# Six row buffers, earlier token numbers and four zero products in the capacity MoE of a four-layer block

## What is computed

```python
logits = x @ gate_weight.T                        # 128 experts
logits = where(old_to_new == -1, -inf, logits)    # 48 are kept
top_v, top_i = top_k(softmax(logits), 8)
top_v = top_v / sum(top_v)
pos = (running count of the tokens of the same expert) - 1
valid = pos < 96                                  # CAP slots for each expert
xb[e, pos] = x[token]                             # gather
h = silu(xb @ Wg[e]) * (xb @ Wu[e])               # 96 inner columns
out = h @ Wd[e]
final[token] += out[e, pos] * weight * valid      # combine
```

## Time and profile before

| what | value |
| --- | --- |
| median of 3 runs | 1504.42 us |
| the profiled execution's own time | 1502.56 us |
| its span, first to last instruction | 1500.7 us |
| PE busy | 1265.7 us (84%) |
| DVE busy | 1178.3 us (79%) |
| ACT busy | 758.1 us (51%) |
| POOL busy | 762.9 us (51%) |
| mean granted TensorE clock | 0.789 |
| layer 3's quads, first to last silu (ACT L1573) | 727.37 to 854.78 us of the span |

### The profile page before, as it was taken

One profiled execution on the slowest core, in us unless ns is written; L12 is line 12 of the kernel. 1 busy time (PEld: TensorE's weight loads), 2 busy tenths in 40 slices (PEclk: granted clock), 3 DMA queues, 4 the chain that ended last, 5 costly groups with the idle time before them and its releaser, 6 DMA issues.

```text
span 1500.7 us, 30682 instructions
## 1 busy us (share of the span) xinstructions
PE 1265.7 (84%) x11448; PEld 778.8 (52%) x11448; DVE 1178.3 (79%) x2410; ACT 758.1 (51%) x1457; POOL 762.9 (51%) x727
## 2 busy tenths in 40 slices
PE   6878999999996999974798873888888889993798
PEld 3544555555553333233687761555555655562455
DVE  7858777777769999977787569888888767659784
ACT  4442222222236988863343334988999943331432
POOL 5444767676611005000332246988988947773262
PEclk9999999999997555557799995555555589996899
DMA  6120111111013999981556524998999921110010
GB/s 215 43 78 32 43 52 42 52 42 52 21 36 65 173 180 174 176 168 41 142 173 173 162 50 84 143 152 145 149 151 150 141 71 40 46 54 31 12 33 28
DMA packets 350670, 143.14 MB, mean 95 GB/s; under 512 B 328912, under 2 KB 331472, under 8 KB 349776
## 3 DMA queue, kind: packets, MB, share of 16 engines
q1 hardware_dynamic: 347232, 132.88, 42.7%
q0 software_dynamic: 1728, 4.72, 1.1%
q10 hardware_dynamic: 1584, 3.86, 0.8%
HBM read 59.09 MB, written 2.10 MB: 41 GB/s over the span
## 4 chain that ended last, share of the span: by engine, by line
PE 50%; DVE 27%; POOL 6%; ACT 5%; issue 5%; DMA 5%; SPq 1%; ACTq 0%; POOLq 0%; DVEq 0%
PE s_all L863 32%; DVE small L2250 7%; PE bank L863 6%; PE s_all L1072 2%; PE bank L1072 2%; POOL c_hi L772 2%; PE s_all L1254 2%; DVE stats L1791 1%; DVE small L2253 1%; POOL c_hi L770 1%; POOL c_lo L772 1%; PE s_all L977 1%; DVE ffbuf L2092 1%; PE bank L1389 1%; DVE xt_lo L1812 1%
## 5 line engine op out<-in xcount | busy, mean ns | idle before, releaser
L619 POOL TENSOR_TENSOR w_hi<-w_in,ws_col 128x768 f16<-128x768 f32 (+1 forms) x76 | 109.6, 1442 | 268.4 <-PE bank L863 259.5
L863 PE MATMUL s_all<-xt_hi,w_hi 128*128 128x512 f16 x576 | 172.5, 381 | 17.2 <-DVE ffbuf L2061 7.1
L2063 DVE TENSOR_TENSOR hid_lo<-ffbuf,hid_hi 128x512 f16<-128x512 f32 x80 | 142.2, 1778 | 56.4 <-ACT hid_hi L1501 56.4
L620 POOL TENSOR_SCALAR w_in<-w_in 128x768 f32<-128x768 f32 (+1 forms) x76 | 182.8, 2405 | 0.0
L1501 ACT ACTIVATE hid_hi<-ffbuf 128x512 f16<-128x512 f32 x80 | 50.4, 630 | 247.8 <-DVE ffbuf L2061 247.8
L863 PE MATMUL s_all<-xt_lo,w_hi 128*128 128x512 f16 x576 | 172.8, 382 | 0.0
L863 PE MATMUL s_all<-xt_hi,w_lo 128*128 128x512 f16 x576 | 172.4, 381 | 0.0
L1639 ACT ACTIVATE ag<-s_all,small 128x1024 int16<-128x1024 f32 x128 | 154.0, 1203 | 23.8 <-DVE small L2253 13.5
L2250 DVE TENSOR_REDUCE small<-s_all 128x1 f32<-128x1024 f32 x128 | 155.5, 1215 | 7.3 <-PE s_all L1254 7.2
L665 POOL DMA_INDIRECT sel<-rows,slot_misc x36 | 43.4, 1204 | 204.9 <-DVE slot_misc L1949 130.6
L1254 PE MATMUL s_all<-ag 32*128 32x512 f16 x256 | 131.5, 616 | 12.2 <-ACT ag L1639 7.4
(11 more groups left out here) (387 smaller groups left out, 3210.9 us busy)
## 6 DMA issues: line engine op xcount, KB each, us to landing
w_in<-in_w_blocks SPq DMA_DIRECT2D x76, 384.0 KB, 3.0
w_in<-in_w_experts SPq DMA_DIRECT2D x48, 320.0 KB, 4.8
region<-in_w_attn SPq DMA_DIRECT2D x4, 512.0 KB, 10.4
sel<-in_k_sel ACTq DMA_DIRECT2D x1, 1280.0 KB, 5.5
ag<-ag SPq DMA_TRANSPOSE x66, 3.4
x<-in_x_in SPq DMA_DIRECT2D x1, 1024.0 KB, 4.9
region<-in_ctxt SPq DMA_DIRECT2D x1, 1024.0 KB, 9.8
ffbuf<-in_mask ACTq DMA_DIRECT2D x1, 1024.0 KB, 5.4
```

Source lines behind the costliest of these rows:

```text
L619: nc.gpsimd.tensor_tensor(hi, w, ws_col[:, 0:1].broadcast_to([P, used]), ALU.mult).then_inc(s_g, 1)
L620: nc.gpsimd.tensor_scalar(w, w, WS, None, ALU.mult).then_inc(s_g, 1)
L863: m = nc.tensor.matmul(outp, lhs, rhs, start=(first and n == 0), stop=(last and n == len(steps) - 1), skip_group_check=True)
L2063: nc.vector.tensor_tensor(hid_lo[:, h, :], hid[:, h, :], hid_hi[:, h, :], ALU.subtract).then_inc(s_hl, 1)
```

## The change

Three edits, all in layer 3.

1. ROW_BUFS goes from 4 to 6. The two new buffers are the first 1024 float16 of `xt_hi`, the high part of the transposed activations, which layer 3 has used for the last time in its router and which layer 4 writes anew. The formula of the wait is unchanged, so all three chunks of quad q now wait until quad q-2 is turned.
2. DVE writes the token numbers right after L1928, ahead of its wait for `m_cum`, not after `key3`.
3. PE multiplies zeros four times (128x128 by 128x512, into bank 0, which gate_up(0) overwrites) between `map_weights` and gate_up(0).

```diff
-ROW_BUFS = 4
+ROW_BUFS = 6
...
-        x_rows = [sel[:, o + n * 2 * D:o + (n + 1) * 2 * D] for n in range(ROW_BUFS)]
+        x_rows = [sel[:, o + n * 2 * D:o + (n + 1) * 2 * D] for n in range(4)] + \
+                 [xt_hi[:, 0, n * 2 * D:(n + 1) * 2 * D] for n in range(2)]
...
                 map_weights()
+                for _ in range(4):
+                    nc.tensor.matmul(bank[0][:, :], zeros16[:, 0:P], zeros16[:, :], start=True, stop=True,
+                                     skip_group_check=True)
                 for q in range(QUADS):
...
                 link(nc.vector.tensor_scalar(one3, new, 1.0, None, ALU.min))
+                for t in range(NT):
+                    m = nc.vector.tensor_scalar(wsplit[:, t, 2 * 64:3 * 64], zeros16[:, 0:64], token[:, 0:1], float(P * t),
+                                                ALU.add, ALU.add)
+                link(m)
                 dve.wait_ge(m_cum, 1)
...
-                for t in range(NT):
-                    m = nc.vector.tensor_scalar(wsplit[:, t, 2 * 64:3 * 64], zeros16[:, 0:64], token[:, 0:1], float(P * t),
-                                                ALU.add, ALU.add)
-                link(m)
                 one_hot(0)
```

## The result

The change took 1490.61 us, the median of nine runs (1485.61 to 1498.50), against 1505.86 us before (nine runs, 1502.71 to 1509.28). The ratio is 0.9914 with a 95% interval of 0.9895 to 0.9933, a gain of 10 to 16 us. The forecast was 1487.9 us, or a gain of 16.5: right in direction and range, some 3 to 4 us too large.

A forecast was written before the change was run, and what follows sets the result against it. Bound: layer 3's ring of gather and turn. Gains of 14.9 (buffers), 1.2 (token numbers) and 0.4 us (zero products), 16.5 in all, take 1502.56 to 1486.1; with 1.86 for the median, 1487.9 us, range 1483 to 1495.

The forecast's parts named there:

- The bound: Layer 3's quads: gathers wait for the previous quad's turn, a ring of 12.1 us per quad that six buffers cut.
- The new pace: Silu 2 to 11 in layer 3: steps alternating 9.68 and 10.51 us, 89.9 us against 104.81, 14.9 us gained.
- So PE and DVE set the pace: Layer 3's quads with the ring cut: PE and DVE limit the steps, a pair costing 20.2 us.
- Rival A: Layer 3's quads: the ring is cut but the new index-to-product chain binds; at +5 us, 1496 us; chance 0.11.
- 3.5 us of slack: Quad 4 of layer 3: rows ready for gate_up at 764.3, PE free only at 767.79, 3.5 us later.
- Rival B: Layer 3's gathers: GpSimd held up in every one beside DVE, 2.04 us more each; 1501 us; chance 0.03.
- Token numbers: Layer 3's prologue: eight writes leave the path between key3 and one_hot(0); 1.2 us gained, bounds 1.1 and 1.3.
- Zero products: PE ahead of gate_up(0): hidden in idle time, cost nothing, may raise the clock; 0.4 us gained, between 0 and 1.7.
- Clock of the combines: First combine of layer 3: started cold, left as it is, with 1.5 us either way for the range.

The follow-up runs named there:

- e1: The change with the six buffers alone, without early token numbers and zero products: 1494.41 us, ratio 0.9944 against the kernel before.
- e3: The change with four row buffers, so early token numbers and zero products alone: 1503.60 us, ratio 1.0006 against the kernel before.
- e4: The change with GpSimd's five memsets for layer 4 held until DVE has written the last turned one-hot matrix: 1489.14 us, ratio 0.9911.
- e8: The kernel e4 without the four zero products: 1490.76 us, ratio 0.9923 against the kernel before.
- e9: The kernel e4, zero products kept, with four fewer fill products ahead of layer 3's transposes: 1489.99 us, ratio 0.9901.
- e12: The change once more, unaltered, to see its spread: 1492.72 us, ratio 0.9918 against the kernel before.
- e5: The kernel e4 with eight products adding zeros to the accumulators after gate_up(1), ahead of the first combine: 1486.37 us, ratio 0.9902.
- e2: The change without the four zero products: 1490.78 us, ratio 0.9924 against the kernel before.
- e6: The kernel e8 with eight products adding zeros ahead of the first combine and eight ahead of the last: 1487.69 us, ratio 0.9896.
- e10: The kernel e8 with four more fill products ahead of layer 3's transposes: 1493.25 us, ratio 0.9925.

## Why the prediction was right, and where not

- **The bound** was named rightly: gather and turn formed a ring of 12.1 us. With it cut (e1) silu 2 to 11 fell by 12.8 us, with it restored (e3) it came back.
- **The new pace.** "89.9 us against 104.81" rested on alternating steps of 9.68 and 10.51. They came as 9.68 and 10.46, and with the memsets out of the way (e4, e8) the whole stretch took 89.6. This term was right to 0.3 us, for the pieces that it looked at.
- **The step that failed** is "So PE and DVE set the pace" for the end of the stretch, where silu 2 to 11 took 92.72 us and not 89.9. I asked what comes late when the gathers come early, but only up to the product. POOL, done with its gathers, goes on to the next work in its program, and that collided with DVE: 2.2 us in the steps 9 to 10 and 10 to 11.
- **Rival A's mechanism** was there too, in one quad. The "3.5 us of slack" held while the chain from index to product was 13.3 us; in quad 9 it took 17.2, the slack was gone, and gate_up started 0.87 late, the sign that I had named for A. Already in quad 4 the turn began 5.2 us after the last gather's issue and not 4.4.
- **Rival B's mechanism** was there, the other way round. I had weighed what DVE does to GpSimd's gathers; after the first (1.99) they took 0.94 to 1.44 us in the change, somewhat more than the 0.95 I took, and it cost nothing. The harm came from GpSimd's memsets to DVE.
- **Token numbers, "1.2 us gained".** The turn's issue did come 1.16 us sooner in the change's profile. The term was right as far as that issue. In ten of the twelve profiles with the early token numbers the issue came 33.8 to 35.0 us after the norm; in e9 and e12 it came after 36.4 and 36.1, no sooner than without them (36.14 before, 36.25 in e1), so other things in the prologue move as much as the term.
- **Zero products, "they cost nothing", "0.4 us".** Wrong in sign. Their engine time was hidden, as forecast (PE still idled 1.28 us after them), but their instructions are four more, and with them an instruction packet came into the turn: gate_up(0)'s rows landed about 1.0 us later on the mean (3.37 to 3.69 without the packet, 4.13 to 4.86 with it). Nor did they warm gate_up(0): from its start to the silu took 4.11 to 4.12 us where it was cold, and less in only two of seven profiles with the zeros (e5, e9) and in three of seven without (e2, e6, e10).
- **Clock of the combines**, named as 1.5 us either way: the first lost 1.6 (silu 0 to 2, 24.19 for 22.60), the last gained 1.6 (17.32 for 18.90).

Sum for layer 3: forecast 16.5; the memsets and the late turn of quad 9 take 2.8 away (92.72 for 89.9), the prologue 1.6, and the two combines cancel: 12.1. That the combines cancel is luck: in e12 both ran cold, silu 2 to 11 and the prologue were 1.1 and 1.4 us longer, and layer 3 gained only 8.0.

Open: what makes the gathers and the turn of quad 9 slow enough to land 0.87 to 1.88 us after PE is ready in the change, e2 and e9 (steps of 10.6 to 11.6), and not in e4 and e8; and what sets the prologue's length, 44.6 to 47.6 us.

## What to carry to other kernels

When buffers that free a producer let it run ahead, follow that engine to the end of its list: the work that it reaches sooner can cost its neighbour more than the engine's own time says. Here the ring of dependent transfers ended only when no member waited for the previous round (four and five buffers 102.6 to 104.8, six 89.6 to 95.3), and not in proportion to the buffers. Compare a stage by its own start and end marks, since here layers that weren't touched moved the total by several us.

## What the runs showed of the hardware

- Beside five memsets of GpSimd, three one-input float16 instructions of DVE (128x1024) took 5.42 to 5.44 us and not 1.27, in all four profiles in which they met; with the memsets moved (e4 and others) they took 1.27. The first of the three, begun 0.17 us before the memsets, alone took 4.66 us in the change and ended 0.3 us after the last memset: it was held through all five and not only through one. Beside the same memsets, DVE's L1972 (two SBUF inputs, one of them float32) took 3.03 us and 3.02 elsewhere. The Trainium skill, "GPSIMD Engine Reference", section "Specifications", names both kinds, a two-port mode and two SBUF inputs, as contending with GpSimd. No run shows which mode L1973 ran in; two SBUF inputs alone, as L1972 has them, did not suffice here.
- One instruction packet (queue q8, about 0.02 MB) coincided with a DMA transpose landing 0.4 to 1.5 us later in seven profiles of fourteen, and moved with the number of PE instructions ahead of it (e9, e10), not with the zero products.
